# Attention and linear-attention stages of a fused transformer kernel: places of side pieces in two hand-written plans

## The chip, the cores and the metric

One core of a Trainium2 chip runs the whole kernel in one launch. Its engines are TensorE (PE in the profile; PEld is its weight load), the vector engine (DVE), ScalarE (ACT), GpSimd (POOL) and SyncE (SP), which issues most DMA transfers. Each engine works through its own queue in order and waits on semaphores for the others. The metric is the time of one execution on the device in microseconds (us), as the median of the runs shown.

## The reference

The input x is [4, 1024, 128] in float32. It passes six residual blocks, each behind a layer norm:

```
x = x + 0.5 * ffn(layernorm(x), W_r, W_k, W_v, mu_r, mu_k)      # token mix: sigmoid(r) * (relu(k)**2 @ W_v)
x = x + attention(layernorm(x), qkv_w, qkv_b, proj_w, proj_b)   # 16 heads of 8, rotary, softmax over 1024 keys
x = x + 0.5 * ffn(layernorm(x), ...)
x = x + 0.5 * moe(layernorm(x), ...)                            # rms norm, top 2 of 8 experts, hidden 256
x = x + linear_attention(layernorm(x), Wq, bq, Wk, bk, Wv, bv, Wo, bo)
x = x + 0.5 * moe(layernorm(x), ...)

# linear_attention, per head, causal:
q, k = softplus(q), softplus(k)
kv, k1 = cumsum(k[:, :, None] * v[:, None, :]), cumsum(k)
out = (q @ kv) / sum(q * k1)
```

## The kernel before, in words

**Tiles.** The 4096 tokens are 32 tiles of 128. Four tiles make a *group* (512 columns, one PSUM bank), eight a *batch* (one sequence). The stages follow each other: a start (first token mixes, queries of batch 0), attention, the expert loops of the first mixture (r = 0, 1), linear attention, the expert loops of the second (r = 2, 3). x stays in SBUF throughout.

**Attention** (`plan_attention`, line 296) is 256 turns and 2 more to drain. A turn makes scores of four heads by one key tile (TensorE, L979), ScalarE takes the exponential of them in two instructions of 1024 columns (L1257), and the weighted sums of the turn follow two turns later (L994). Scores rotate over six PSUM banks, the weighted sums collect in bank 6, which the vector engine copies out every 16 turns (L1224, "the sums' copy"). What else there is to do is cut into *pieces*, which the planner lays into the turns: queries and keys of the next batch (`norm`, `xt`, `rot`, `split`, `norms`), the bound and the maxima that the exponential needs (`bound`, `max`), values (`val`), division and projection (`div`, `turn`, `proj`, `stats`), the second token mix (`mn`, `mt`, `mk`, `mr`, `mv`, `ms`; `md` and `mx` are its parts on GpSimd and the vector engine), norm factors (`factors`) and the router (`rroot` to `rweight`, then `scat`, the scatters of tokens to expert slots). All products of pieces share one PSUM bank, bank 7, so a product waits until the product before it has been read out.

`turn_of` (line 184) takes the head piece of each of the first two works in the list, and at most one that is a product; a piece ("rest",) fills a turn with nothing. Each engine's queue holds the pieces of a turn in the order of `out`. `attention_queries` (111) puts the i-th `split` of a batch into the turn of another work's product. A split is seven instructions of the vector engine on 128x512 (`dve_attention_side`, line 1067, in batches 1 to 3: square L1096, sums, casts and subtractions L1112, L1113 twice, L1115); they cut the rotated queries or keys into bfloat16 parts. A copy out of the bank of a token mix's transposes is L804 (`mt`). The bound (`attention_maxima`, 141; `dve_bound`, 1167) is a short chain of small vector instructions, then a product (L919), then another.

**Linear attention** (`plan_linear`, 377) is 128 steps and 4 more, 16 to a group of four tiles: a step is one tile by one of four head groups. Scores go to banks 0 to 3 (L1969 and L1965), the mask to lin_scores on the vector engine (L2098), the output to banks 4 and 5 (L1982). All other products take banks 6 and 7 in turn, so each of them waits until the product two before it has been read out. Each step has four lists, issued in this order: *before* (`lnorm`), *state* (`lstate`, the running kv sum, L2045 and L2049 of the vector engine), *out* (one or two pieces of `linear_prepare` and `linear_finish`) and *extra* (the mixture's gathers `gath` and additions `cadd`, `lfac`, router and scatters). `linear_prepare` (159) makes the next group: transposes `lxt` (L597 from `lnorm`'s output), projections `lz` and `lv`, softplus `lexp`, `lln`, sums `lsum`, mask, transposed keys `lkt`. `linear_finish` (174) divides a tile (`ldiv`, L2057 and L2058) and, behind a group's fourth tile, turns it (`lturn`), projects (`lproj`, added to x on GpSimd, L2196) and takes statistics (`lstats`).

`lnorm` normalises the four tiles of a group (`dve_normalise`, L586). `lfac` makes the norm factors of some groups from their statistics (`dve_norm_factors`, L575 to L578, through the Newton steps of `dve_inverse_root`, L561). `route_part` (236) is `rroot` (another inverse root, L1452), `rnorm` (eight tiles scaled, L1463), `rext` (transposes) and `rscore`; `route_slots` (247) is `rtop` (masks of the best two, L1479 to L1488), `rcount` (products L1426 and L1427), `rscan`, `rplace`, `roff`, `rweight`. `spread` (258) lays them out over steps with `ROUTE_TURNS` empty steps behind each kind. From `rplace` on one scatter (L1601, GpSimd) is issued per step.

Of the kernel before, what the change touches and what calls it, by code (L numbers as in the profile page):

```python
# [25 lines left out]
TPB = SEQ // P  # L26
BANK = 512
TPG = BANK // P
# [53 lines left out]
GATHER_STEPS = (9, 4)  # L82
ROUTE_TURNS = {"rroot": 1, "rnorm": 2, "rext": 1, "rtop": 1, "rcount": 1}
PAD = P // HPG
# [56 lines left out]
def attention_maxima(b):  # L141

    yield OTHER, ("rest",)
    yield PRODUCT, ("bound", b)
    yield OTHER, ("rest",)
    yield PRODUCT, ("max", b)
# [27 lines left out]
def linear_finish(u):  # L174
    g, c = divmod(u, TPG)
    yield PRODUCT, ("ldiv", u)
    if c == TPG - 1:
        yield PRODUCT, ("lturn", g)
        yield PRODUCT, ("lproj", g)
        yield OTHER, ("rest",)  # L180
        yield OTHER, ("lstats", g)
# [76 lines left out]
def spread(pieces):  # L258

    out = []  # L260
    for piece in pieces:
        out += [piece] + [None] * ROUTE_TURNS.get(piece[1][0], 0)
    return out
# [32 lines left out]
def plan_attention(k):  # L296
# [11 lines left out]
    for n in range(len(A_STEPS) + A_LAG):  # L308
        out, sums = [], None
        for work in begin.get(n, []):  # L310
            works.insert(len(works) if work[0][1][0] in ("norm", "factors", "mn") else 0, work)
        out = turn_of(works)
        done.update(out)
# [63 lines left out]
def plan_linear(k):  # L377
# [6 lines left out]
    later = {}  # L384
    for at in range(HALF):
        for c in range(TOPK):
            n = GATHER_STEPS[0] * (TOPK * at + c) // GATHER_STEPS[1]
            later.setdefault(n, []).append(("gath", 1, at, c))
        later.setdefault(n + 4, []).append(("cadd", 1, at))
        if at % TPG == TPG - 1:  # L390
            later.setdefault(n + 5, []).append(("cstat", 1, at // TPG))
            if at // TPG % 2:
                later.setdefault(n + 6, []).append(("lfac", 1, at // TPG - 1, 2))
    routes, scatters = [], []
# [10 lines left out]
    for n in range(len(L_STEPS) + L_LAG):  # L405
        before, state, sums = [], None, None
        if n < len(L_STEPS):
# [5 lines left out]
            if not preparing and prepared + 1 < GROUPS and n >= STEPS_PER_GROUP * (prepared - 1) + L_START * HEAD_GROUPS:  # L413
                prepared += 1
                preparing = list(linear_prepare(prepared))
                works.append(preparing)
                before.append(("lnorm", prepared))
            u = g * TPG + c
# [18 lines left out]
        if ("lstats", 1) in out:  # L437
            routes += spread(route_part(2, 0, TPB))
        if ("lstats", HALF_GROUPS - 1) in out:
            routes += [None] * 3 + spread(route_part(2, 1, TPB)) + spread(route_slots(2))  # L440
        if ("lstats", HALF_GROUPS + 1) in out:
            routes += spread(route_part(3, 0, TPB))
        if ("rplace", 2) in extra:
# [2152 lines left out]
```

## Time and profile before

| | |
|---|---|
| runs of the kernel before | 1348.8, 1349.03, 1354.61 us; median 1349.03 |
| the profiled execution's own time | 1345.49 us, with a span of 1343.5 and a granted TensorE clock of 0.899 |
| busy in the span | TensorE 1084.8 us (81%), vector engine 657.9 (49%), ScalarE 807.0 (60%), GpSimd 376.6 (28%) |
| start | 0 to 96.4 us |
| attention | 96.4 to 661.6 us |
| expert loops 0 and 1 | 661.6 to 865.8 us |
| linear attention | 865.8 to 1128.6 us |
| expert loops 2 and 3 | 1128.6 to 1343.5 us |

Times are microseconds unless they are marked ns. A window's row gives a stretch, its length, and the busy time and number of instructions of each engine; PEclk is the TensorE clock that the chip granted in it, as a share of full speed. In a timeline, the bracket behind an instruction is the time that its engine stood idle just before it, and the instruction of another engine that ended the wait. L12 is line 12 of the kernel.

### The profile page before, as it was taken

The page shows a single profiled execution, that of the slowest core. Times are in us where ns is not written, and L with a number is a line of the kernel's source. Part 1 is how long each engine was busy: PE and PEld are TensorE (multiplying, and loading weights), DVE is VectorE, ACT ScalarE, POOL GpSimd, SP SyncE. Part 2 cuts the span into 40 slices and gives each one's busy share as a digit, 9 for nine tenths or more (in the row PEclk, how much of TensorE's full clock was granted, in tenths as well). Part 3 has the DMA queues.
Part 4 walks back from the last instruction along what each step waited for, and adds up shares of the span by engine and source line. Part 5 has one row for each costly group of instructions (what it writes and reads, how often), then busy time and mean ns, then how long its engine had stood idle before and what let it go on. Part 6 is the DMA issues. An engine that isn't in the chain of part 4 may idle for free.

```text
span 1343.5 us, 20969 instructions
## 1 busy us (share of the span) xinstructions
PE 1084.8 (81%) x7616; PEld 504.0 (38%) x7616; DVE 657.9 (49%) x2060; ACT 807.0 (60%) x1164; POOL 376.6 (28%) x376
## 2 busy tenths in 40 slices
PE   3459899899999999999879399787887776898940
PEld 2332222222322321232256256444544344565630
DVE  5752554456355340433165157667666663633522
ACT  4328788688898899989735255644443331464520
POOL 2100111111110102333003643243331263155535
PEclk8679999899999999999999789889888686898975
DMA  4360450432036502100012233100000001143522
GB/s 139 57 96 1 65 90 1 71 57 27 1 56 96 155 1 76 54 15 30 13 40 85 81 87 93 31 17 17 12 14 1 15 33 38 50 118 99 141 66 66
DMA packets 83411, 74.07 MB, mean 55 GB/s; under 512 B 11248, under 2 KB 77680, under 8 KB 82416
## 3 DMA queue, kind: packets, MB, share of 16 engines
q1 hardware_dynamic: 73824, 55.06, 18.8%
q0 software_dynamic: 8192, 16.79, 4.3%
q8 instruction: 66, 1.08, 0.4%
q10 hardware_dynamic: 1296, 0.86, 0.2%
q14 instruction: 33, 0.27, 0.1%
HBM read 39.26 MB, written 33.42 MB: 54 GB/s over the span
## 4 chain that ended last, share of the span: by engine, by line
PE 53%; DVE 20%; ACT 11%; issue 6%; POOL 3%; DMA 2%; another core or an unknown queue 0%; SPq 0%; POOLq 0%; DVEq 0%; ACTq 0%
PE ps L994 11%; PE ps L1666 9%; ACT attn_probs L1257 8%; PE ps L979 6%; PE ps L1692 4%; PE ps L597 3%; PE ps L888 2%; PE ps L1969 2%; POOL moe_back L1611 2%; PE ps L1678 2%; PE ps L1893 1%; DVE lin_scores L2098 1%; PE ps L1656 1%; DVE stats L554 1%; PE ps L1982 1%
## 5 line engine op out<-in xcount | busy, mean ns | idle before, releaser
L1257 ACT ACTIVATE attn_probs<-ps 128x1024 f32<-128x1024 f32 x512 | 485.7, 1075 | 86.0 <-PE ps L979 85.8
L994 PE MATMUL ps<-attn_probs,attn_v 128*18 128x512 f32 x2048 | 273.9, 607 | 5.7 <-DVE room L1224 5.1
L979 PE MATMUL ps<-stack 50*128 50x512 bf16 x1024 | 167.1, 391 | 17.3 <-DMA stack<-row_maxima 11.4
L1601 POOL DMA_INDIRECT slots<-moe_xr,moe_slot x128 | 125.3, 979 | 196.3 <-ACT attn_probs L1257 81.1
L1611 POOL DMA_INDIRECT moe_back<-results,moe_slot x128 | 123.9, 968 | 110.7 <-PE ps L1656 46.8
L1666 PE MATMUL ps<-stack,lin_scores 128*128 x312 | 153.8, 616 | 0.0
L979 PEld LDWEIGHTS ps<-stack 50*128 50x128 bf16 x1024 | 34.1, 94 | 253.6 <-ACT attn_probs L1257 226.3
L1767 ACT ACTIVATE lin_scores<-ps 128x256 f32<-128x256 f32 x156 | 58.6, 382 | 107.0 <-PE ps L1666 101.8
L1740 DVE TENSOR_TENSOR lin_scores<-ps,lin_scores 128x256 f32<-128x256 f32 x156 | 59.0, 418 | 103.5 <-ACT lin_scores L1767 85.2
L1692 PE MATMUL ps<-stack,lin_scores 128*128 x624 | 85.6, 281 | 8.9 <-ACT lin_heads_out L1780 6.8
L1692 PEld LDWEIGHTS ps<-stack,lin_scores 128*128 128x128 f32 x624 | 77.7, 195 | 10.7 <-issue 10.5
L1295 POOL TENSOR_TENSOR room<-room 128x512 f32<-128x512 f32 x16 | 24.5, 1530 | 186.2 <-DVE room L1089 186.2
L1666 PEld LDWEIGHTS ps<-stack,lin_scores 128*128 128x128 f32 x312 | 55.6, 199 | 39.8 <-issue 39.8
L2098 DVE TENSOR_TENSOR lin_scores<-ps,c_causal 128x512 f32<-128x512 f32 x64 | 41.1, 683 | 49.5 <-PE ps L1969 46.8
L1733 DVE TENSOR_SCALAR lin_scores<-ps,c_norm_scale 128x256 f32<-128x256 f32 x80 | 37.8, 473 | 54.1 <-PE ps L1656 48.5
L994 PEld LDWEIGHTS ps<-attn_probs,attn_v 128*18 128x18 f32 x2048 | 34.9, 96 | 75.9 <-issue 46.8
L1089 DVE SCALAR_TENSOR_TENSOR room<-ps,c_attn_b,moe_xr 128x512 f32<-128x512 f32 x32 | 23.9, 748 | 79.9 <-PE ps L888 78.4
L2168 ACT ACTIVATE lin_scores<-ps 128x512 f32<-128x512 f32 x64 | 34.8, 594 | 45.8 <-PE ps L1969 45.5
L1656 PE MATMUL ps<-c_ident,moe_gathered 128*128 128x128 f32 x156 | 33.0, 294 | 30.7 <-DMA moe_gathered<-slots 18.7
L1773 ACT ACTIVATE lin_scores<-ps 128x512 f32<-128x512 f32 x80 | 46.8, 584 | 14.9 <-PE ps L1678 8.4
L1678 PEld LDWEIGHTS ps<-c_ident,lin_scores 128*128 128x128 f32 x312 | 39.0, 143 | 37.5 <-issue 36.3
L888 PE MATMUL ps<-room,c_qk_w 128*128 128x256 f32 x128 | 45.3, 458 | 9.2 <-DVE mix_xt L804 8.8
(237 smaller groups left out, 1567.6 us busy)
## 6 DMA issues: line engine op xcount, KB each, us to landing
stack<-qk_parts SPq DMA_DIRECT2D x48, 256.0 KB, 8.9
moe_gathered<-slots SPq DMA_DIRECT2D x76, 128.0 KB
results<-lin_heads_out SPq DMA_DIRECT2D x76, 128.0 KB
slots<-zeros SPq DMA_DIRECT2D x2, 2496.0 KB, 14.9
qk_parts<-moe_xr SPq DMA_DIRECT2D x32, 128.0 KB, 2.7
qk_parts<-moe_xr SPq DMA_DIRECT2D x16, 192.0 KB, 2.8
stack<-in_expert_w SPq DMA_DIRECT2D x1, 3072.0 KB
x<-in_x SPq DMA_DIRECT2D x8, 256.0 KB, 8.2
```

The source lines that it names most:

```text
L888: instruction = T.matmul(k.ps[:, bank, cols], w[:, 2 * qk + which, :], d.xt[:, half * BANK:(half + 1) * BANK][:, cols], start=True, stop=True)
L979: instruction = T.matmul(k.ps[:, SCORE_BANKS[i % 3][s], :], d.stack[b % 2][rows, 1, pair, kt * P:(kt + 1) * P], d.stack[b % 2][rows, 0, pa ...
L994: instruction = T.matmul(k.ps[32 * j:32 * j + STRIP, PV_BANK, :], d.v[:, b % 2, kt, first:first + STRIP], d.probs[:, n % A_PROBS, j * BANK ...
L1257: A.activation(d.probs[:, n % A_PROBS, 2 * e * BANK:2 * (e + 1) * BANK], k.ps[:, banks[0]:banks[1] + 1, :].rearrange("p a n -> p (a n)"), ...
L1601: G.indirect_dma_start(out=k.dram["slots"][half], out_offset=bass.IndirectOffsetOnAxis(ap=d.slot[:, s, at, c:c + 1], axis=0), in_=d.xr[:, ...
L1611: G.indirect_dma_start(out=k.back[:, at % RING, c, :], out_offset=None, in_=k.dram["results"][half], in_offset=bass.IndirectOffsetOnAxis(a ...
L1666: T.matmul(k.ps[:, bank, :], d.gt[:, u % NB, i, :], w[:, bass.ds(offset[u, i], 2 * HIDDEN)], start=True, stop=True).then_inc(k.full[bank], 1)
L1678: instruction = T.transpose(k.ps[:, bank, at:at + P], d.h[:, u % NB, i, c * P:(c + 1) * P], k.ident[:, :])
L1692: instruction = T.matmul(k.ps[:, bank, i * DIM:(i + 1) * DIM], d.ht[:, u % NB, i, c * P:(c + 1) * P], w[:, 2 * HIDDEN + c * DIM:][:, bass. ...
L1740: V.tensor_tensor(d.h[:, u % NB, i, :], k.ps[:, bank, 0:HIDDEN], d.silu[:, u % NB, i, :], ALU.mult).then_inc(k.free[bank], 1)
L1767: A.activation(d.silu[:, u % NB, i, :], k.ps[:, bank, HIDDEN:2 * HIDDEN], ACT_FN.Silu).then_inc(k.e_silu, 1)
L2098: V.tensor_tensor(d.scores[:, m % NS, :].rearrange("p (j t) -> p j t", j=HPG), k.ps[:, bank, :].rearrange("p (j t) -> p j t", j=HPG), caus ...
```

## The change

In the plan of attention: the pieces of a turn are sorted so that a `split` comes last in it, and `attention_maxima` has a second empty turn ahead of `bound`. In the plan of linear attention: an empty turn ahead of `lturn`; `lnorm` of groups 2 to 7 moves from the step in which its group's preparation begins with `lxt` (12, 30, 46, 62, 78, 94) to the one at which two pieces of the preparation before it are left (10, 27, 43, 59, 75, 91); `lfac` moves from the steps behind the statistics of every second group (two calls of two groups) to steps 30, 58 and 81 (groups 0; 1 and 2; 3); the routers' parts begin `ROUTE_WAIT` = 4 steps behind the statistics they need (before: at once, or 3 steps), with other empty steps between the pieces (`rscore` 0, `rtop` 2, `rext` 1, and none behind `rcount`), and one more ahead of `rtop`. `linear_prepare`, the engines' instructions and all buffers stay as they are. The whole diff:

```diff
--- before.py
+++ after.py
@@ -80,7 +80,8 @@
 L_STEPS = [(g, c, gr) for g in range(GROUPS) for c in range(TPG) for gr in range(HEAD_GROUPS)]
 STEPS_PER_GROUP, L_OUT = TPG * HEAD_GROUPS, (4, 5)
 GATHER_STEPS = (9, 4)
-ROUTE_TURNS = {"rroot": 1, "rnorm": 2, "rext": 1, "rtop": 1, "rcount": 1}
+ROUTE_WAIT, ROUTE_TURNS = 4, {"rroot": 1, "rnorm": 2, "rext": 1, "rscore": 0, "rtop": 2}
+FACTORS_AT = {30: (0, 1), 58: (1, 2), 81: (3, 1)}
 PAD = P // HPG
 
 PRODUCT, SAME_BANK, OTHER = "uses the tensor engine", "goes on with its bank", "uses others only"
@@ -140,6 +141,7 @@
 
 def attention_maxima(b):
 
+    yield OTHER, ("rest",)
     yield OTHER, ("rest",)
     yield PRODUCT, ("bound", b)
     yield OTHER, ("rest",)
@@ -175,6 +177,7 @@
     g, c = divmod(u, TPG)
     yield PRODUCT, ("ldiv", u)
     if c == TPG - 1:
+        yield OTHER, ("rest",)
         yield PRODUCT, ("lturn", g)
         yield PRODUCT, ("lproj", g)
         yield OTHER, ("rest",)
@@ -309,7 +312,7 @@
         out, sums = [], None
         for work in begin.get(n, []):
             works.insert(len(works) if work[0][1][0] in ("norm", "factors", "mn") else 0, work)
-        out = turn_of(works)
+        out = sorted(turn_of(works), key=lambda piece: piece[0] == "split")
         done.update(out)
         b = next_batch
         if b < BATCH and n >= STEPS_PER_BATCH * (b - 1) - BATCH_AHEAD and {("max", b - 1), ("val", b - 1, 1, 1), ("factors", b * TPB, (b + 1) * TPB)} <= done:
@@ -389,8 +392,8 @@
         later.setdefault(n + 4, []).append(("cadd", 1, at))
         if at % TPG == TPG - 1:
             later.setdefault(n + 5, []).append(("cstat", 1, at // TPG))
-            if at // TPG % 2:
-                later.setdefault(n + 6, []).append(("lfac", 1, at // TPG - 1, 2))
+    for n, groups in FACTORS_AT.items():
+        later.setdefault(n, []).append(("lfac", 1) + groups)
     routes, scatters = [], []
     ring = 0
 
@@ -414,7 +417,8 @@
                 prepared += 1
                 preparing = list(linear_prepare(prepared))
                 works.append(preparing)
-                before.append(("lnorm", prepared))
+            elif len(preparing) == 2 and prepared + 1 < GROUPS:
+                before.append(("lnorm", prepared + 1))
             u = g * TPG + c
             u = g * TPG + c
             if gr == HEAD_GROUPS - 1 and (u + 1) % TPB:
@@ -435,11 +439,11 @@
         if routes and (one := routes.pop(0)):
             extra.append(one[1])
         if ("lstats", 1) in out:
-            routes += spread(route_part(2, 0, TPB))
+            routes += [None] * ROUTE_WAIT + spread(route_part(2, 0, TPB))
         if ("lstats", HALF_GROUPS - 1) in out:
-            routes += [None] * 3 + spread(route_part(2, 1, TPB)) + spread(route_slots(2))
+            routes += [None] * ROUTE_WAIT + spread(route_part(2, 1, TPB)) + [None] + spread(route_slots(2))
         if ("lstats", HALF_GROUPS + 1) in out:
-            routes += spread(route_part(3, 0, TPB))
+            routes += [None] * ROUTE_WAIT + spread(route_part(3, 0, TPB))
         if ("rplace", 2) in extra:
             scatters = transfers("scat", 2)
         fill(extra)
```

## Rows read from the trace of the kernel before

**Rows 1.** Windows: a stretch, its length, busy us of PE, PEld, DVE, ACT, POOL, PEclk, DMA.

```profile
96.40:661.60 565.20, 529.75 (x3719) 149.58 (x3715) 239.85 (x699) 492.84 (x530) 95.34 (x84) 0.98 0.24 47
...
865.80:1128.60 262.80, 206.16 (x2124) 118.30 (x2124) 167.98 (x507) 108.05 (x191) 100.34 (x102) 0.83 0.06 18
```

**Rows 2.** Timeline of attention turn 15 to 17: start, us, engine, line, operation, wait before.

```profile
130.13 1.65 POOL L1295 TENSOR_TENSOR room<-room 128x512 f32<-128x512 f32 x1 [7.18 <-DVE room L1089]
...
130.57 1.50 DVE L1112 CAST moe_xr<-room 128x512 bf16<-128x512 f32 x1
...
130.72 0.66 PE L597 MATMUL ps<-c_ident,moe_gathered 128*128 128x128 f32 x4
...
134.36 0.68 DVE L804 COPY mix_xt<-ps 128x512 f32<-128x512 f32 x1
...
138.24 1.02 ACT L1257 ACTIVATE attn_probs<-ps 128x1024 f32<-128x1024 f32 x1 [3.58 <-PE ps L979]
```

**Rows 3.** Timeline of ScalarE, the exponentials behind the splits of turns 22, 59, 65.

```profile
156.41 1.02 ACT L1257 ACTIVATE attn_probs<-ps 128x1024 f32<-128x1024 f32 x1 [2.48 <-PE ps L979]
...
240.46 1.02 ACT L1257 ACTIVATE attn_probs<-ps 128x1024 f32<-128x1024 f32 x1 [3.55 <-PE ps L979]
...
256.37 1.94 ACT L1257 ACTIVATE attn_probs<-ps 128x1024 f32<-128x1024 f32 x2 [3.04 <-PE ps L979]
```

**Rows 4.** Timeline of TensorE, the bound's product in batches 1 and 3.

```profile
188.31 0.41 PE L919 MATMUL ps<-attn_by_head,ones_f 128*128 128x32 f32 x2 [1.73 <-DVE attn_by_head L1183]
...
424.81 0.41 PE L919 MATMUL ps<-attn_by_head,ones_f 128*128 128x32 f32 x2 [2.62 <-DVE attn_by_head L1183]
```

**Rows 5.** Windows of the linear stage, 16 steps each, from step 16 on.

```profile
883.90:913.10 29.20, 24.60 (x284) 13.58 (x276) 20.95 (x58) 14.69 (x26) 13.57 (x14) 0.94 0.08 20
913.10:951.80 38.70, 28.72 (x279) 16.18 (x282) 28.02 (x95) 15.33 (x27) 12.82 (x13) 0.78 0.04 11
951.80:985.50 33.70, 29.68 (x289) 17.28 (x292) 20.75 (x57) 15.22 (x27) 12.32 (x13) 0.85 0.07 17
985.50:1020.90 35.40, 24.59 (x275) 13.82 (x277) 26.57 (x93) 14.74 (x26) 8.87 (x9) 0.89 0.03 6
1020.90:1062.50 41.60, 32.15 (x292) 18.18 (x291) 26.29 (x78) 15.93 (x28) 6.95 (x7) 0.75 0.01 3
1062.50:1094.00 31.50, 23.70 (x273) 13.62 (x276) 22.07 (x65) 14.69 (x27) 19.57 (x20) 0.88 0.09 31
1094.00:1122.50 28.50, 24.06 (x276) 15.05 (x271) 9.70 (x29) 8.19 (x15) 17.94 (x21) 0.86 0.11 36
```

**Rows 6.** Waits of TensorE in the linear stage: waited for, us in total, times, longest.

```profile
PE ps L597 <- DVE room L586: 13.7, 5, 7.3
PE ps L1965 <- DVE lin_scores L2098: 11.6, 8, 4.9
PE ps L597 <- DVE lin_heads_out L2058: 7.5, 8, 3.0
PE ps L1426 <- DVE moe_both L1488: 6.2, 1, 6.2
...
PE ps L597 <- issue: 2.4, 1, 2.4
```

**Rows 7.** Timeline of the vector engine ahead of `lnorm 6`.

```profile
1008.59 0.17 DVE L578 TENSOR_SCALAR ln_var<-moments 128x8 f32<-128x8 f32 x1
...
1015.84 1.11 DVE L586 TENSOR_SCALAR room<-x,moments,ln_rstd 128x128 f32<-128x128 f32 x4
```

**Rows 8.** Windows: steps 20 to 30 of the linear stage, and the five or so behind.

```profile
893.10:910.50 17.40, 14.08 (x162) 8.30 (x162) 16.64 (x47) 8.52 (x15) 8.71 (x9) 0.90 0.06 15
910.50:922.20 11.70, 10.42 (x103) 5.18 (x103) 3.37 (x9) 6.33 (x11) 3.34 (x4) 1.00 0.08 21
```

**Rows 9.** Timeline: the last scatter, and expert loop 2's first product.

```profile
1123.44 0.96 POOL L1601 DMA_INDIRECT slots<-moe_xr,moe_slot  x1 [1.32 <-PE ps L1982]
...
1136.19 0.63 PE L1656 MATMUL ps<-c_ident,moe_gathered 128*128 128x128 f32 x2
```

## The prediction

> **What bounds the kernel now.** The profiled execution spans 1343.5 us and took 1345.49; the runs have a median of 1349.03 (1348.8 to 1354.61). The sum below is made against the profiled execution, which lies 3.5 under the median, and the forecast is the median less the same saving.
>
> I read the busy time by stretch first [rows 1]. The attention stage (565 us) keeps ScalarE busy for 493 with its exponentials: it is the bound there, so a microsecond is saved only where ScalarE stands idle. The linear stage (263 us) has no full engine: TensorE works 206, the vector engine 168, and TensorE's clock is 0.83 of full. Both work through hand-written queues in order, so that stage is bound by waits. Then I read who idles before what.
>
> Attention, turn 15 (the turn of a `split` and the transposes `mt 0`) [rows 2]: TensorE has made the transposes by 131.4, but the vector engine does the split's square, casts and subtractions first (the row of the first cast begins at 130.57), and only at 134.36 copies `mt` out of the one spare PSUM bank. TensorE waits for that bank with `rot`, comes late with the next scores, and ScalarE idles 3.58 us. The same pattern costs 2.48 at turn 22, 3.55 at turn 59 and 3.04 at turn 65 [rows 3]. At turn 81 a wait has another cause: there the copy of the weighted sums stands behind the split, and the product beside it (`mr`) is read by ScalarE. At the bound, TensorE waits 1.73 us (batch 1) and 2.62 us (batch 3) for the short vector chain that makes the bound's operand [rows 4].
>
> Linear stage, by groups of 16 steps [rows 5]: 29.2 us without router work, 38.7, 33.7, 35.4 and 41.6 where chains are laid in, then 31.5 and 28.5. What ends the waits of this stage on TensorE [rows 6]: 13.7 us in five waits for normalised tokens, the longest 7.3 for `lnorm 6`, which is issued in the very step of its transposes `lxt 6`; 11.6 in eight for a score bank that the vector engine frees late, the longest 4.9 in the group from 913.10; 7.5 in eight for the division's output or its bank; 6.2 for `rtop`'s masks, which `rcount` multiplies. The rows of the vector engine show what stood ahead of `lnorm 6` [rows 7]: from 1008.59 the factor chain (2.64 us), then mask, division and root chain (4.6 together), and at 1015.84 `lnorm` itself (1.1). The clock falls with such a wait: the group of the 4.9 has a granted clock of 0.78, that of the 6.2 one of 0.75, the first 0.94 [rows 5].
>
> **The change, part by part.**
>
> *Split last in its turn.* No instruction is added. Turn 15: the copy of `mt` (0.68) ends at 132.1, `rot` no longer waits. The split now runs 132.1 to 135.6 (its seven instructions without the POOL addition of 1.65 us that stretched the first cast to 1.50 [rows 2]); behind it come rotation (about 0.7, as the copy), `mn` (1.1, as `lnorm` in rows 7) and the sums' copy (0.7), which ends near 138.2. TensorE needs it there for its weighted sums of turn 18 and no longer waits: gain 3.7, the idle of 3.58 and a little behind it. Turn 22, without a sums' copy: gain 2.3. Turn 59: gain 3.8, as at turn 15. Turn 65: the sums' copy still stands behind the split, which now begins only after the copy of `mt 3`, so it ends half a microsecond later: loss 0.4; the 3.04 stays. Turns 28 and 78 put the copy of `mk` first, where the next turn is empty on TensorE anyway; the split ends about 2 us later, POOL's square now falls on the cast, and the sums' copies at 33 and 81 come 1 us later: loss 1.0 each.
>
> *Second empty turn.* Its place in the plan decides. For batch 1 it falls beside the division of turn 35: the bound stays at turn 38 directly behind the vector engine's work for `proj`, and its 1.73 stays. For batch 2 `mk 3` fills it, again a copy right ahead of the chain: nothing, at most 0.3 at `max`. All later pieces move by one turn, `mn 4` then stands behind a factor chain and a statistics, and `mt 4` waits 1 us more: loss 1.0. For batch 3 all moves by two to four turns: the bound comes at turn 144 with 2 turns' time for `mn 7` and `mx 6`, and its 2.62 goes. But `split 3 3` now stands at turn 139 behind factors (2.5) and `mn 6` (1.1), and `mt 6`'s copy behind it: TensorE waits 2.5 us at turn 141 and 1.0 at turn 140 instead. Net gain 1.2. The router's chains and scatters move by two turns, where ScalarE does not wait for them: nothing; if that cover were gone, 1 to 2 us.
>
> Sum of attention: 3.7 + 2.3 + 3.8 - 0.4 - 2.0 - 1.0 + 0.3 + 1.2 = 7.9, say 8. Bounds: 12 (the four first waits, 12.6 us, all go) and 3.
>
> One price is open: POOL's subtraction `md` (about 1 us) now starts just as the split's square does. The rows show a cast held 1.50 us beside a POOL addition [rows 2]. The Trainium skill (SBUF — State Buffer, Who interferes with whom) says that an instruction of the vector engine with two SBUF inputs, as the square is, is blocked whole by a GpSimd one that was first; by it turns 15 and 59 would each give about 1 us less and the sum would be 33 instead of 35. The rows agree for the cast; I leave the square free.
>
> *Linear stage.* The empty turn ahead of `lturn` takes away its wait of 0.3 us for the division in seven groups, and puts `proj`'s addition one place back in the vector queue. The first `lsum` comes ahead of it. `lnorm` moves three steps ahead of `lxt`: that wait goes, but `lnorm` (1.03 to 1.1) now stands ahead of the addition that frees the bank for `lkt`, two products later. Two factor chains of two groups become three (1, 2, 1): one chain of 2.64 more. `rroot` and `rnorm` move to steps where the vector queue is short: [rows 8] it is busy 16.64 of 17.4 us in steps 20 to 30 of a group, and 3.37 of 11.7 behind them. `rtop` moves from steps 87 and 89 to 90 and 93, `rcount` from 91 to 96.
>
> I walked each group through both queues in the new order with the durations of the rows; every product waits for the bank of the product two before it. Against [rows 5]:
> - Steps 16 to 31: the vector queue is full from step 20, and the chain of one group at step 30 follows `lxt`. 29.2 becomes 28.2.
> - 32 to 47: `lfac`, `rroot` and `rnorm` are gone from steps 39 to 43. The 4.9, 3.2 for `lnorm 4` (of the 13.7), `rext` (1.0, goes on into the next group) and about 3 of half clock go, 3 us of bank waits return. 38.7 becomes 29.3.
> - 48 to 63: takes in that router work (3 us of TensorE), and at step 58 a factor chain just ahead of `lnorm 5`, so `lkt 4` waits 3.1 for its bank. 33.7 becomes 34.1.
> - 64 to 79: the 7.3, 0.3 and 1 of clock go; behind statistics twice, an add-back and `lnorm` the banks of `lkt` and `lxt` come 2.8 later. 35.4 becomes 29.6.
> - 80 to 95: the 6.2, 1.9 for `lnorm 7` (of the 13.7) and about 3 of half clock go; `lfac` at 81 makes `rext` wait 1.9, and bank waits of 1 return. 41.6 becomes 33.2.
> - 96 to 111: three waits of together 6 behind `rroot` and `rnorm` (the 2.4 that rows 6 put down to issue, and parts of the 11.6 and 7.5) and 2 of half clock go; `rcount` to `rweight` (7 us of vector work) bring 2.7 back. 31.5 becomes 26.2.
> - 112 to 127: half clock at its head goes. 28.5 becomes 25.5.
>
> That is 32.5. A walk does not see every semaphore; I take 27 and keep 33 and 12 as ends. The scatters end 4 steps later: last issue at 1123.44 before, TensorE's first product with their result at 1136.19 [rows 9], 12 us apart; the linear stage's last division, turn and projection cover the delay of some 5 us. If that cover went, 5 us.
>
> Sum: 8 + 27 = 35. Profiled execution 1310.5, median **1314**.
>
> **The rivals.**
>
> *Waits change their place.* In the linear stage the vector engine is full in steps 20 to 30 of each group with or without the change, and what is taken from the head of its queue comes back at `lkt` and `lxt`. For it: 16.64 of 17.4 us [rows 8]. Against it: the 7.3 and 6.2 have whole chains ahead of them that now lie where it is idle 8 of 11.7. Gain then 12 in the linear stage and 5 to 8 in attention: 1331.
>
> *TensorE keeps its clock.* If all groups ran at 0.94 and no bank wait were new, each would come near 28 with its router work: 33 to 35 there and 12 in attention, 1303. For it: in the first group nothing but 4.6 us is idle. Against: `lnorm` stands ahead of the bank's addition. The Trainium skill (TensorE: Matmul & The Clock Gate, HAM oscillation) says that repeated waits bring the engine down to half clock again and again; the clocks of 0.75 and 0.78 in rows 5 agree.
>
> *Slower: the vector queue is the bound of the whole stage.* Then no removed wait counts and what is added does: `lnorm` ahead of the state sum in five groups (5.2), the third chain (2.6), later sums in attention (2.0 + 0.4), the chain ahead of `mt 6` (1), scatters uncovered (5): 16 slower, 1365. It decides once the vector engine is busy in steps 31 to 35 too; it is so for 29% there [rows 8].
>
> *The change does not do what it says* holds in part (the empty turn of batches 1 and 2) and is in the sum; if only the linear half worked, 1322.
>
> **How the numbers follow.** Main case 0.60 (its own range 1305 to 1324), waits change place 0.22, TensorE keeps its clock 0.11, slower 0.03, about no change 0.04. The range reaches from 1301 to 1331: it takes in the main case and most of its neighbours. A measurement of this kernel tells about 0.5% from no change, 6.7 us: faster 0.92, same 0.05, slower 0.03.
>
> **What would show it.** ScalarE's idle of 3.58, 2.48 and 3.55 us gone, that of 3.04 still there or longer; TensorE's wait of 1.73 at the bound of batch 1 still there, a new one of 2 to 3 us at `norms` of batch 3. In the linear stage the 4.9, 7.3 and 6.2 gone, new waits of 1 to 3 us of `lkt` and `lxt` for banks freed by the state sum and division, groups of 26 to 34 us, a granted clock over 0.88. Wrong, if `lkt` waits over 4 us in most groups, if the clock stays at 0.83, or if TensorE waits for the gathered rows at the head of the third expert loop.

## The result and the profile after

The changed kernel takes **1333.61 us** (median of 4 runs, 1330.94 to 1334.21), the kernel before 1349.43 on the same chip. The ratio is 0.9884 with an interval of 0.9862 to 0.9905: faster by 15.8 us, where 35 were forecast; 1333.61 lies 2.6 us above the upper end of the range. The two profiled executions are 1334.21 and 1345.49 us, only 11.3 apart; terms below are read from their traces.

The page of the changed kernel, its head and the costliest group:

```profile
span 1332.3 us, 20939 instructions
...
PE 1076.1 (81%) x7574; PEld 506.0 (38%) x7616; DVE 652.0 (49%) x2073; ACT 806.3 (61%) x1164; POOL 373.7 (28%) x376
...
L1261 ACT ACTIVATE attn_probs<-ps 128x1024 f32<-128x1024 f32 x512 | 485.7, 1074 | 86.0 <-PE ps L983 85.8
```

ScalarE waits 86.0 us ahead of its exponentials, exactly what the page of before shows for that group. So attention has gained nothing as a whole. The windows of its four areas (attention, expert loops 0 and 1, linear stage, expert loops 2 and 3) say where the 11 us are; columns as in rows 1:

```profile
96.50:661.10 564.60, 526.40 (x3701) 148.81 (x3707) 237.24 (x699) 492.71 (x530) 94.83 (x84) 0.98 0.24 48
661.10:868.20 207.10, 163.31 (x838) 107.52 (x840) 104.99 (x367) 94.52 (x219) 71.48 (x74) 0.90 0.24 69
868.20:1117.50 249.30, 200.95 (x2104) 121.66 (x2131) 164.97 (x520) 108.28 (x192) 98.46 (x102) 0.86 0.06 17
1117.50:1332.30 214.80, 144.09 (x745) 97.47 (x745) 83.94 (x256) 80.78 (x195) 92.50 (x97) 0.83 0.31 87
```

With the same edges (first exponential, end of the last one, first output product of the linear stage, and 2.3 to 2.6 us behind the end of its last one) the kernel before has 564.3, 205.1, 265.7 and 212.0. Attention is level, the linear stage gives 16.4, and the expert loops, whose code is the same, take 2.0 and 2.8 back. The 2.8 is no more than two executions of one kernel differ by: the kernel before again (e11) has 215.7 there.

**Attention.** ScalarE's timeline of the changed kernel, behind the splits of turns 15, 22 and 59 (the three that [rows 2, 3] show with 3.58, 2.48 and 3.55 us of idle time), then turns 93 and 99:

```profile
134.53 1.94 ACT L1261 ACTIVATE attn_probs<-ps 128x1024 f32<-128x1024 f32 x2 [0.21 <-PE ps L983]
...
150.42 1.94 ACT L1261 ACTIVATE attn_probs<-ps 128x1024 f32<-128x1024 f32 x2 [0.21 <-PE ps L983]
...
232.15 1.94 ACT L1261 ACTIVATE attn_probs<-ps 128x1024 f32<-128x1024 f32 x2 [0.21 <-PE ps L983]
...
316.77 1.94 ACT L1261 ACTIVATE attn_probs<-ps 128x1024 f32<-128x1024 f32 x2 [4.86 <-PE ps L983]
...
332.57 1.94 ACT L1261 ACTIVATE attn_probs<-ps 128x1024 f32<-128x1024 f32 x2 [3.44 <-PE ps L983]
```

The three waits are gone. By turn 64 the changed kernel is 8.8 us ahead. It loses 4.9 of that at turn 93 and 3.1 at turn 99, where the kernel before did not wait at all. From turn 86 to turn 104 the net loss is 6.6. What stands ahead is seen in the timeline of turns 90 to 93:

```profile
307.44 0.17 DVE L582 TENSOR_SCALAR ln_var<-moments 128x8 f32<-128x8 f32 x1
...
307.64 1.27 DVE L567 TENSOR_SCALAR ln_bits<-ln_var 128x8 int32<-128x8 int32 x1
...
312.10 1.08 DVE L590 TENSOR_SCALAR moe_gathered<-x,moments,ln_rstd 128x128 f32<-128x128 f32 x4
313.10 0.16 DVE L582 TENSOR_SCALAR ln_var<-moments 128x8 f32<-128x8 f32 x1
313.24 1.11 PE L601 MATMUL ps<-c_ident,moe_gathered 128*128 128x128 f32 x4 [3.40 <-DVE moe_gathered L590]
...
315.47 0.69 DVE L808 COPY mix_xt<-ps 128x512 f32<-128x512 f32 x1
...
316.13 1.04 PE L983 MATMUL ps<-stack 50*128 50x512 bf16 x4
```

From 307.44 the vector engine works through `factors 0 8` (begun behind a product, and 3.5 us long), statistics (1.2) and `mn 4` (1.0); TensorE waits 3.40 us for `mn 4` with its transposes `mt 4`. Then the vector engine does `factors 24 32` before it copies `mt 4` out of the spare bank. In the plan before, `mt 4` was issued one turn ahead of `factors 24 32`; the empty turn put both into turn 92, the chain first. Turn 99 is the same kind of thing, in the timeline from 326 on:

```profile
326.49 2.56 DVE L590 TENSOR_SCALAR room<-x,moments,ln_rstd 128x128 f32<-128x128 f32 x4
...
328.98 0.68 DVE L1228 COPY room<-ps 128x512 f32<-128x512 f32 x1
329.11 1.04 PE L601 MATMUL ps<-c_ident,room 128*128 128x128 f32 x4 [1.74 <-DVE room L590]
...
330.80 1.10 DVE L590 TENSOR_SCALAR room<-x,moments,ln_rstd 128x128 f32<-128x128 f32 x4
```

`norm 3 0` is in turn 97 as before, but its transposes `xt 3 0`, which before came at turn 104, now find a free turn at 98, right behind it. They wait for it, and the sums' copy (L1228) stands behind half of it.

Two things make both waits longer than the order alone. GpSimd works beside what stands ahead: the `ln_bits` instruction of `factors 0 8` takes 1.27 us beside an addition of GpSimd from 307.61 to 308.88 (0.17 in e1, where no such addition runs beside it, and 1.26 or 1.27 in e2, e5 and e10), and the first half of `norm 3 0` takes 2.56 beside two instructions of GpSimd, where its second half takes 1.10. This is read from the timelines; no run takes GpSimd's work away there. And behind each wait TensorE's eight products of the weighted sums take 1.91 us instead of 1.05.

**Linear stage**, the windows that answer to [rows 5], groups of 16 steps from step 16 on:

```profile
886.40:913.90 27.50, 22.24 (x276) 13.36 (x275) 21.93 (x70) 14.48 (x26) 13.48 (x14) 1.00 0.08 18
913.90:944.50 30.60, 25.97 (x270) 15.52 (x275) 22.97 (x76) 14.84 (x26) 11.90 (x14) 0.83 0.07 16
944.50:978.50 34.00, 26.90 (x285) 16.26 (x288) 24.28 (x78) 15.92 (x28) 12.85 (x13) 0.94 0.07 17
978.50:1009.40 30.90, 24.70 (x267) 14.24 (x271) 22.04 (x72) 14.72 (x26) 8.50 (x9) 0.89 0.03 8
1009.40:1046.40 37.00, 31.93 (x289) 19.76 (x295) 24.05 (x77) 16.01 (x28) 5.10 (x5) 0.78 0.00 1
1046.40:1072.80 26.40, 22.70 (x266) 13.85 (x271) 22.32 (x67) 13.63 (x25) 12.74 (x13) 0.87 0.06 19
1072.80:1106.40 33.60, 27.27 (x279) 16.86 (x279) 14.59 (x52) 8.69 (x16) 20.10 (x24) 0.85 0.10 35
1106.40:1117.50 11.10, 6.22 (x64) 4.64 (x53) 0.56 (x3) 1.19 (x2) 6.54 (x7) 0.70 0.15 49
```

| steps | before | forecast after | after |
|---|---|---|---|
| 16 to 31 | 29.2 | 28.2 | 27.5 |
| 32 to 47 | 38.7 | 29.3 | 30.6 |
| 48 to 63 | 33.7 | 34.1 | 34.0 |
| 64 to 79 | 35.4 | 29.6 | 30.9 |
| 80 to 95 | 41.6 | 33.2 | 37.0 |
| 96 to 111 | 31.5 | 26.2 | 26.4 |
| 112 to 127 | 28.5 | 25.5 | 33.6 |
| 128 to 131 | 9.0 | (as before) | 11.1 |

Up to step 111 the walk is off by 1.3 us or less in all groups but one, where 3.8 remain. The last group is 8 us too long. The waits of TensorE in the stage answer to [rows 6]:

```profile
PE ps L601 <- DVE lin_total L2053: 7.0, 5, 2.7
PE ps L601 <- DVE lin_heads_out L2062: 5.9, 5, 3.0
PE ps L1969 <- DVE lin_scores L2102: 5.7, 4, 1.9
...
PE ps L1933 <- issue: 4.1, 1, 4.1
PE ps L1933 <- ACT lin_sums L2180: 3.6, 2, 2.9
```

The waits of 4.9, 7.3 and 6.2 us are gone, and new ones of `lkt` and `lxt` for a bank that the state sum frees (7.0 in five) stand in their place, the longest 2.7. Those were in the walk. The 4.1 and 2.9 in the last two rows lie behind step 112 and were not. The kernel before has the like there; these are waits in its steps 112 to 131:

```profile
ACT lin_sums L2176 <- remote: 6.2, 1, 6.2
PE ps L1929 <- issue: 3.6, 1, 3.6
```

"remote" means that nothing of this core that the profile shows ended the wait.

### The profile page after: what moved, and what is told of

It reads as the page before. It is cut to its first block, busy times and chain, and to the rows that moved or that the text cites. A ratio compares the mean times of both kernels' runs of the same rounds, so it can differ in the third digit from the quotient of the medians.

```text
span 1332.3 us, 20939 instructions
## 1 busy us (share of the span) xinstructions
PE 1076.1 (81%) x7574; PEld 506.0 (38%) x7616; DVE 652.0 (49%) x2073; ACT 806.3 (61%) x1164; POOL 373.7 (28%) x376
## 4 chain that ended last, share of the span: by engine, by line
PE 55%; DVE 18%; ACT 10%; issue 6%; POOL 3%; DMA 2%; another core or an unknown queue 2%; SPq 0%; POOLq 0%; DVEq 0%; ACTq 0%
PE ps L998 12%; PE ps L1670 9%; ACT attn_probs L1261 8%; PE ps L983 6%; PE ps L1696 4%; PE ps L601 3%; PE ps L892 2%; PE ps L1682 2%; POOL moe_back L1615 2%; PE ps L1973 2%; DVE lin_scores L2102 2%; PE ps L1986 1%; PE ps L1660 1%; PE ps L1897 1%
## 5 line engine op out<-in xcount | busy, mean ns | idle before, releaser
L998 PE MATMUL ps<-attn_probs,attn_v 128*18 128x512 f32 x2048 | 275.7, 611 | 10.2 <-DVE room L1228 7.3
L1784 ACT ACTIVATE lin_heads_out<-ps 128x256 f32<-128x256 f32 x80 | 30.1, 376 | 39.0 <-PE ps L1696 21.3
```

The source lines that it names most:

```text
L998: instruction = T.matmul(k.ps[32 * j:32 * j + STRIP, PV_BANK, :], d.v[:, b % 2, kt, first:first + STRIP], d.probs[:, n % A_PROBS, j * BANK ...
```

## The experiments

Ratios are to the kernel before, timed on the same chip beside the run. The chips differ: the kernel before took 1329.81 us on the chip of e1 to e4, 1329.38 on that of e5 to e8 and 1348.15 on that of e9 to e12 ("the slow chip" below). So ratios are compared, and stretches of traces.

### e1: split last, alone

```diff
-        out = turn_of(works)
+        out = sorted(turn_of(works), key=lambda piece: piece[0] == "split")
```

> The kernel before with the split sorted to the end of its turn, and nothing else. Theory (sort pays, the extra empty turn loses): ScalarE's waits of 3.6, 2.5 and 3.6 us at turns 17, 24 and 61 fall to 0.2, those of about 1.5 at turns 93 and 0.4 at turn 99 stay as before; the attention stage is 8 us shorter, 1341. Rival (the later vector work of the sorted turns is what makes the new waits of 4.9 and 3.4 us): these two are here, the stage is no shorter at turn 104 than before, 1349.

1317.96 us, ratio **0.9918** (0.9895 to 0.9941). Attention of this kernel, of the kernel before (e11), and of the changed one again (e5), each from its first exponential to its last:

```profile
96.00:650.10 554.10, 522.71 (x3711) 148.52 (x3707) 236.43 (x699) 492.66 (x530) 94.77 (x84) 0.99 0.25 48
```

```profile
95.90:657.30 561.40, 523.36 (x3700) 149.27 (x3707) 239.88 (x699) 492.52 (x530) 95.39 (x84) 0.98 0.24 48
```

```profile
96.40:656.50 560.10, 522.28 (x3701) 148.83 (x3707) 237.38 (x699) 492.63 (x530) 95.05 (x84) 0.98 0.24 48
```

The split alone gains 7.3 us against e11, 10.2 against the first trace of before (564.3) and 10.9 against e3, which has the old plan of attention and ran on the same chip (565.0). Such differences carry 3 to 5 us that have nothing to do with the plan: two traces of one plan can differ by 1.5 us at turn 68 and again at turn 83 (before and e11, the changed kernel and e5, e4 and e1). The waits at turns 17, 24 and 61 are 0.21, turns 93 and 99 have none, as before. The theory holds; the new waits do not come from the sort.

### e2 and e10: the empty turn, alone and for batch 2 only

e2 is the kernel before with one line in `attention_maxima`; e10 has the sorted split, and the line only for batch 2:

```diff
     yield OTHER, ("rest",)
+    yield OTHER, ("rest",)
     yield PRODUCT, ("bound", b)
```

```diff
     yield OTHER, ("rest",)
+    if b == 2:
+        yield OTHER, ("rest",)
     yield PRODUCT, ("bound", b)
```

> The kernel before with the second empty turn ahead of the bound alone. Theory: the pieces of batch 2 and all behind them move by a turn, mt 4 stands behind two factor chains and mn 4 (wait of about 5 us at turn 93), norm 3 0 stands ahead of the sums' copy and xt 3 0 (3.4 us at turn 99); gained are 1.1 at the bound of batch 2 and about 0.5 in batch 3. Net 7 us slower, 1356. Rival (my prediction's step): within 1 us of the kernel before, 1349, with mt 4 only 1 us later.

> The kernel with the split sorted last alone, and the second empty turn only for batch 2. Theory (one turn's shift of mt 4 behind two factor chains and of norm 3 0 ahead of xt 3 0 is the whole loss): waits of 4.9 us at turn 93 and 2 to 3.4 us at turn 99, attention 6 to 8 us longer than with the split alone, ratio 0.997. Rival (the loss adds up from the empty turns of all three batches): under 3 us longer, 0.993.

e2: 1339.93 us, ratio **1.0084** (1.0057 to 1.0110), 10.1 us slower, attention 571.3 us (565.0 in e3 on the same chip):

```profile
95.70:667.00 571.30, 530.97 (x3711) 149.82 (x3707) 240.56 (x699) 492.17 (x530) 95.26 (x84) 0.97 0.24 47
```

It has the wait at turn 93 with 3.32 us, one of 2.1 at turn 99, and one of 6.49 at turn 141: `split 3 3` has come into the turn of `mn 6` and, with nothing sorted, stands ahead of it, so that TensorE waits 5.0 us for `mn 6` at the transposes `mt 6`. e10: 1353.06 us, ratio **1.0027** (1.0005 to 1.0048), against 0.9918 for the split alone. One empty turn in one batch gives all of the gain back. Its two waits, in ScalarE's timeline at turns 93 and 99:

```profile
315.33 1.94 ACT L1259 ACTIVATE attn_probs<-ps 128x1024 f32<-128x1024 f32 x2 [4.86 <-PE ps L981]
331.13 1.94 ACT L1259 ACTIVATE attn_probs<-ps 128x1024 f32<-128x1024 f32 x2 [3.37 <-PE ps L981]
```

They are those of the changed kernel (4.86 and 3.44). The loss between turns 86 and 104 is 6.7 us in e10, 6.6 in the changed kernel's first trace and 6.0 in e5; all kernels with the sorted split and no empty turn lose nothing there. So the rival, that the loss adds up over three batches, falls. e10 ended 0.6% above its expected ratio. Attention was 565.9 us, 11.8 over e1: beside the 6.7 there are 3.2 at turns 67 to 84, of the kind that differs between traces of one plan, and 2.4 behind turn 104. Expert loops 0 and 1, behind it, took 209.7 us against 201.8; e9 and e12, with e1's plan of attention, had 208.2 and 205.4 there on the same chip as e10, so about half or more of that part is no matter of the plan.

### e3: the linear half alone; e4: all but the empty turn; e5: the changed kernel again

e3 is the diff of the change without its two edits of attention; e4 is the changed kernel with this:

```diff
     yield OTHER, ("rest",)
-    yield OTHER, ("rest",)
     yield PRODUCT, ("bound", b)
```

> The whole edit of the linear stage without that of attention. Theory (halves add up): the linear stage is 16 us shorter, its last 20 steps are 5 to 7 us longer than in the kernel before, 1333. Rival (the stalls of the last 20 steps of the changed kernel were chance in one execution): the stage is 23 us shorter, 1326.

> The changed kernel without the second empty turn ahead of the bound. Theory: split last saves 8 and the linear stage 16, nothing is given back at turns 93 and 99: 1325, 8 us under the changed kernel. Rival (the empty turn is neutral and something else costs turns 93 and 99): 1333.

> The changed kernel once more, for its profile beside the others. Theory (sort -10, empty turn +7 to +9, linear half -20, additive): ratio to the kernel before 0.985; its last 20 steps of the linear stage without the long stalls that the first profile shows in them (34 us from step 112 on, not 45). Rival (the stalls belong to the changed plan): 45 us there again, ratio 0.988 or more.

e3: 1309.45 us, ratio **0.9845** (0.9817 to 0.9872). e4: 1302.83, **0.9803** (0.9771 to 0.9835). e5: 1310.73, **0.9864** (0.9829 to 0.9899). Sort, empty turn and linear half multiply to 0.985, the changed kernel has 0.9864 here and had 0.9884 first: the parts add up. e3's and e4's absolute expectations were written for the first chip; their ratios come out at 0.984 and 0.980 instead of 0.988 and 0.982. e3's own trace, on the chip of e1 and e2 (257.1 us in both), has a linear stage of 237.3 us, 19.8 less:

```profile
866.60:1103.90 237.30, 203.24 (x2139) 120.76 (x2136) 165.52 (x522) 108.68 (x192) 95.99 (x100) 0.87 0.06 17
```

Its last 20 steps take 34.2 us at a granted clock of 0.76 in steps 112 to 127, where e1 has 29.0; that is what the theory expected (5 to 7 more), but without the "remote" waits of the first trace. e4's stage, the same step list on the same chip, is 226.3.

The tail of the linear stage in e5, steps 112 to 127 and 128 to 131:

```profile
1066.20:1089.10 22.90, 20.17 (x276) 13.75 (x276) 14.96 (x51) 8.45 (x16) 18.82 (x21) 1.00 0.15 48
1089.10:1094.90 5.80, 4.58 (x69) 3.55 (x62) 1.16 (x5) 1.19 (x2) 4.43 (x6) 1.00 0.15 48
```

28.7 us, where the first trace of the same program has 44.7. On this chip the whole stage is 231.9 us, and 257.1 in e1, which has the old linear plan and ran on another fast chip: 25.2 saved, close to the 27 forecast. Here the gain is taken back elsewhere, at the head of expert loop 2. TensorE's first product there, in e5 and then in e1:

```profile
1104.34 0.69 PE L1660 MATMUL ps<-c_ident,moe_gathered 128*128 128x128 f32 x2 [6.08 <-DMA moe_gathered<-slots]
```

```profile
1112.72 0.44 PE L1656 MATMUL ps<-c_ident,moe_gathered 128*128 128x128 f32 x2 [1.35 <-DMA moe_gathered<-slots]
```

The wait for gathered rows grew from 1.35 to 6.08 us, and loops 2 and 3 from 206.6 to 211.3: the scatters end four steps later in a stage that ends sooner. The other runs on the fast chips agree: 3.7 to 7.1 us of this wait and 209.1 to 211.3 us in the loops with the late scatters (e3, e4, e5, e6, e8), 1.4 and 206.6 to 207.5 with the early ones (e1, e2, e7).

The same step list also does not always take the same time: in e4 it ran in 226.3 us, 5.6 less than in e5. The difference is a clock that fell further in e5 than in e4, in the groups of steps 32 to 47 and 80 to 95. These are the two groups in e4:

```profile
904.60:932.80 28.20, 24.32 (x273) 13.58 (x273) 21.98 (x72) 14.84 (x26) 11.34 (x12) 0.94 0.06 17
...
997.30:1031.30 34.00, 29.56 (x289) 17.61 (x288) 24.28 (x77) 15.92 (x28) 5.10 (x5) 0.87 0.00 1
```

28.2 and 34.0 us at granted clocks of 0.94 and 0.87; e5 has 30.6 and 36.9 at 0.83 and 0.78, the changed kernel's first trace the same as e5, and e3 nearly so. So most of the 3.8 us that were missing in steps 80 to 95 are a fall to the lower of the clock's two levels (1.2 GHz of 2.4), not a wait that the walk had missed. No run tells why e4 was spared it.

The test of the empty turn inside the changed kernel is e4 against e5. They ran on two chips, their intervals touch (0.9835 and 0.9829), and e4's attention took 559.1 us, only 1.0 less than e5's: e4 has the longer waits at turns 39, 68 and 83. Against the changed kernel's first ratio (0.9862 to 0.9905) e4 is apart, and in the turns from 86 to 104 it loses nothing where e5 loses 6.0.

### e6, e7, e8, e12: the parts of the linear edit, each undone in e4

```diff
# e6: lnorm in the step of lxt
+                before.append(("lnorm", prepared))
-            elif len(preparing) == 2 and prepared + 1 < GROUPS:
-                before.append(("lnorm", prepared + 1))
# e7: router as before
-ROUTE_WAIT, ROUTE_TURNS = 4, {"rroot": 1, "rnorm": 2, "rext": 1, "rscore": 0, "rtop": 2}
+ROUTE_TURNS = {"rroot": 1, "rnorm": 2, "rext": 1, "rtop": 1, "rcount": 1}
...
# e8: two chains
-FACTORS_AT = {30: (0, 1), 58: (1, 2), 81: (3, 1)}
+FACTORS_AT = {39: (0, 2), 74: (2, 2)}
# e12: no empty turn ahead of lturn
     if c == TPG - 1:
-        yield OTHER, ("rest",)
         yield PRODUCT, ("lturn", g)
```

> The kernel of the run without the empty turn, with lnorm back in the step of its transposes lxt. Theory (the long wait for lnorm 6 came from the factor and root chains ahead of it, which stay moved): lxt waits 1 to 2 us in five groups, 5 us slower than that run (its ratio was 0.980), 0.984. Rival (the place of lnorm is what removed the 7.3 us wait): a wait of over 4 us at lxt 6 is back and the ratio is 0.990.

> The kernel of the run without the empty turn, with the router's pieces at their old waits and spacings (about four steps sooner). Theory: root chain and eight-tile scaling fall into the full steps of the vector queue, and rcount comes two steps behind the last masks: waits at the score banks of steps 44 to 46 and 76 to 80, and 3 us or more at rcount; 8 us slower than that run, 0.986. Rival (the factor chains' move did it): within 3 us of it, 0.981.

> The kernel of the run without the empty turn, with the factors in two chains (steps 39 and 74, two groups each) in place of three. Theory: group 32 to 47 is 3 us longer, group 64 to 79 2 us longer (a chain straight ahead of lnorm 6), group 48 to 63 3 us and group 80 to 95 1 us shorter: within 2 us, 0.981. Rival (the vector queue's total decides): a chain less makes it 2.6 us faster, 0.978.

> The kernel of the run without the empty turn, without the empty turn ahead of lturn; statistics and router move one step sooner with it. Theory: TensorE waits 0.3 us for the division in seven groups again, the projection's addition stands ahead of the first lsum: 2 us longer in the linear stage, 1 us back from scatters that begin a step sooner: 0.981. Rival (this empty turn is what empties the queue ahead of lkt): 5 us or more longer, 0.985.

| run | median | ratio (interval) | linear stage | loops 2 and 3 |
|---|---|---|---|---|
| e4 | 1302.83 | 0.9803 (0.9771 to 0.9835) | 226.3 | 211.2 |
| e6 | 1305.30 | 0.9826 (0.9789 to 0.9864) | 238.8 | 211.3 |
| e7 | 1298.78 | 0.9766 (0.9732 to 0.9801) | 232.6 | 207.5 |
| e8 | 1299.47 | 0.9764 (0.9729 to 0.9799) | 230.7 | 209.1 |
| e12 | 1318.76 | 0.9783 (0.9760 to 0.9807) | 243.8 (slow chip) | 213.2 |

**e6.** Only the place of `lnorm` differs, and the stage is 7 to 12 us longer than in e5 and e4. `lxt` waits 8.7 us in four groups, in the waits of TensorE in its linear stage:

```profile
PE ps L599 <- DVE room L588: 8.7, 4, 2.9
```

The longest is 2.9 us, not the 7.3 of before: the long one needed the chains ahead of it. The theory has the waits about right (1 to 2 us in five groups expected, 1.65 to 2.94 in four found). By ratio e6 is not told from e4, since their intervals overlap.

**e7** missed its expectation altogether: 0.986 was forecast, 0.977 came. TensorE waits 3.1 us at `rcount` again, though now for a bank that the state sum frees and not for `rtop`'s masks, and the group of steps 32 to 47 takes 33.3 us, so the linear stage is a little longer than in e5. But the scatters start three steps sooner, and loops 2 and 3 take 207.5 us, as with the old plan; its first product there waits 1.43 us for gathered rows:

```profile
1087.41 0.44 PE L1659 MATMUL ps<-c_ident,moe_gathered 128*128 128x128 f32 x2 [1.43 <-DMA moe_gathered<-slots]
```

On the chip as a whole the router's later place earns nothing that these intervals could tell from zero, and may lose. Its group of steps 80 to 95 takes 34.2 us all the same (34.0 in e4, 41.6 before), so most of what the prediction counted there for `rcount` comes without the move. **e8**: two chains or three, no difference that can be told; the order of the groups is as forecast (31.4 for steps 32 to 47, 30.8 for 48 to 63, 32.4 for 64 to 79, 30.8 for 80 to 95). **e12**: no difference that can be told either.

### e9: scatters early

```diff
-            routes += [None] * ROUTE_WAIT + spread(route_part(2, 1, TPB)) + [None] + spread(route_slots(2))
+            routes += [None] * 3 + spread(route_part(2, 1, TPB), SLOT_TURNS) + spread(route_slots(2), SLOT_TURNS)
```

`SLOT_TURNS` has the spacings of before; the rest is e4.

> The kernel of the run without the empty turn, with the second router part and the slots of expert loop 2 (root chain to slot weights) at their old distances, so that the scatters begin three steps sooner; the first part stays four steps later. Theory (the later scatters cost 5 us at the head of expert loop 2): TensorE's wait there for gathered rows falls from 6 to 7 us to 1.4, the last two loops take 207 us and not 211, the linear stage is 227 to 229 us: 5 us faster than the run without the empty turn (0.980) and 2 us faster than the one with the whole router as before (0.977), ratio 0.975. Rival (the router's place in steps 76 to 91 brings back waits of the same size in the linear stage): 0.980.

1317.44 us, ratio **0.9775** (0.9754 to 0.9796), the lowest median on the slow chip and 1.1% under the changed kernel's 0.9884, with intervals that do not touch. But it came to the slow chip, where the wait that it should remove is small anyway (loops 2 and 3 take 213.1 us, 215.7 in e11), so the test of its own point is open: e7 shows that point, not e9. Against e4, e7, e8 and e12 it is not told apart. What beats the changed kernel is what these five share, the missing empty turn in attention.

### e11: the kernel before, again

> The kernel before itself, for its profile beside the others. Theory (the long waits that the first profile has in the last 20 steps of the linear stage belong to that execution or chip and not to the plan): 29 us from step 112 on and not 37.5, linear stage 257 us, last two loops 207, span 1325. Rival (they belong to the plan of before): 37 us there.

1347.23 us, ratio 0.9998 (0.9981 to 1.0015). Its steps 112 to 127 and 128 to 131:

```profile
1091.10:1120.40 29.30, 23.47 (x271) 14.89 (x268) 9.70 (x29) 8.17 (x15) 17.91 (x21) 0.85 0.11 37
1120.40:1128.20 7.80, 7.67 (x61) 5.79 (x61) 1.10 (x4) 1.19 (x2) 0.96 (x1) 0.50 0.28 78
```

37.1 us, as in the first trace of before (37.5); the same linear plan takes 29.0 in e1 and e2, and the changed one 28.7 in e5 against 44.7. All four kernels on the slow chip have a long tail (37.1 to 44.0), and none on the fast ones (28.3 to 34.2, where the longer ones have no such stall but steps at the clock's lower level). My theory said "that execution or chip". The single execution falls, and so does the rival (the plan alone), since the same plan has no such tail on the faster chips. In these traces it goes with the chip, and the plan adds to it: 37.1 to 37.5 with the old plan, 40.2 in e9, 44.0 in e12 and 44.7 in the changed kernel. From step 112 on these plans issue 15, 16, 18 and 19 scatters. Each is a single trace. The timeline of e11 shows such a stall, in which GpSimd goes on and the vector engine does one instruction of 0.20 us:

```profile
1112.83 0.96 POOL L1601 DMA_INDIRECT slots<-moe_xr,moe_slot  x1 [0.31 <-issue]
...
1114.09 0.96 POOL L1601 DMA_INDIRECT slots<-moe_xr,moe_slot  x1 [0.30 <-issue]
...
1116.05 0.60 ACT L2176 ACTIVATE lin_sums<-ps 128x512 f32<-128x512 f32 x1 [6.35 <-remote]
1116.70 1.92 PE L1929 MATMUL ps<-c_head_rows,lin_sums 128*128 128x36 f32 x8 [3.67 <-issue]
```

ScalarE starts a copy 6.35 us after its last work, with nothing of this core named that it waited for, and TensorE's product that reads the copy starts right behind it. The traces of e1 to e8 name no such releaser ("remote") in the linear stage. What it waits for is open; a run on that chip with the scatters taken out of the tail would tell whether they have to do with it, and was not made.

## Why the prediction was wrong

**Split last: right.** The term was 7.4; whole attention stages differ by 7.3 to 10.9 (e1 against e11, before and e3) and by as little as 2.3 (e4 against e11). The turns say it better. Against the first trace of before, the changed kernel gains 8.5 us in turns 16 to 64 and gives 1.4 back by turn 86, for which the forecast had 8.8 and 1.4. Turn 15 went as told: in the changed kernel the split runs from 131.68 to 135.9 (forecast 132.1 to 135.6) and the sums' copy ends at 138.2 (forecast 138.2). The open price came out as taken: the square is 0.68 us long as before, and it is again the first cast that stretches, to 1.25, beside GpSimd's subtraction of 1.41. The Trainium skill (SBUF — State Buffer, Who interferes with whom) says that of an instruction of the vector engine with two SBUF inputs and one of GpSimd that reads SBUF, the one issued first blocks the other whole. The trace agrees: GpSimd's began 0.16 us after the square, and the square kept its 0.68.

**Second empty turn: this step failed.** I wrote "`mt 4` waits 1 us more: loss 1.0" and a net gain of 1.2 for batch 3, +0.5 in all. The traces with it show a loss of 6.0 to 6.7 us between turns 86 and 104 (changed kernel, e5, e10), those without it none. For batch 3, where I had +1.2, the changed kernel loses 1.2 us from turn 112 to 176 in its first trace and gains 0.3 in e5. I had seen that `mn 4` stands behind a chain and missed that `factors 24 32`, with `md 4` before, now shares its turn with `mt 4` and stands between the transposes and their copy out of the bank. And I followed `mt 4` only: `norm 3 0` and `xt 3 0` are pieces of the next batch, which the shift brought from seven turns apart to one. A shift by one turn was priced by its nearest victim; it moves every later meeting of two works.

**Linear stage: the walk was near, the end of the stage was not; this step failed on the chip of the result.** The walk gave 32.5, of which I took 27. On the faster chips it is 19.8 (e3), 25.2 (e5) and 30.8 (e4). On the chip of the result it is 16.4: the last twenty steps, for which the walk had a gain of 3 ("half clock at its head goes"), lost 7.2 (37.5 to 44.7), with stalls that the trace of before shows as well and that the walk left out. That is 10.2 of the 16.1 us that the walk is off. The other 5.8 lie ahead of step 112, 3.8 of them in steps 80 to 95, and these are mostly the clock; the 5.5 that I had taken off the walk cover them.

**Scatters: priced at nothing, with 5 us if the cover went.** It went: 4.7 us on the faster chip (e5 against e1), 2.5 to 4.7 in the five runs with late scatters. I had named it ("if TensorE waits for the gathered rows at the head of the third expert loop"), but the cover had been measured in a stage 25 us longer. On the chip of the result the stalls of the tail left time for the scatters, and the wait is not there.

**The sum.** Against the profiled execution: forecast 8 + 27 + 0 = 35; found 0 + 16.4 - 2.8, less 2.0 in expert loops 0 and 1 and 0.3 elsewhere, = 11.3. By the medians 15.8. The miss is not the slow chip's alone: on e5's chip the same change saves 18.7 us by the medians (1329.38 to 1310.73), with the linear term near its forecast and the empty turn and the scatters against it. The rival *waits change their place* gave 1331, nearest in number; its mechanism did not happen, for steps 32 to 111 gained 22 us. *TensorE keeps its clock* (1303, a ratio of 0.966) came in no run: the lowest ratio is 0.976, and e4's 1302.83 us is near it in number only, on a chip where the kernel before takes 1329.81. *Slower* had the right place in one term, the scatters, and was far off in all.

## What to carry to other kernels

Where a planner deals pieces of several lists into turns, an empty turn is no local edit: print both plans, and for each pair "long vector chain, then a short instruction that frees a bank" compare the distance in turns, for all later works and not just the next. Test such an edit alone; here one line took back what another line had earned, and together they looked like nothing. Compare turn by turn and not stage by stage, since here two traces of one plan differ by up to 5 us in a stage. And when a stage is made shorter, work that was hidden at its end has to be measured against the new length.

## What was not expected of the hardware

- The same program takes 1329 us on some chips and 1348 on others (1.4%). About 8 us of that are in the last 20 steps of the linear stage (29.0 against 37.1), where one scatter per step is issued and ScalarE stands still for up to 6 us with no releaser in the core's own events. Another 5 to 9 are in expert loops 2 and 3 (206.6 and 206.8 us in e1 and e2, 212.0 and 215.7 in the two traces of the kernel before). ScalarE has "remote" waits in the expert loops of all traces from the slower chips (9.6 to 18.7 us at one line) and in none from the faster ones.
- The same attention plan took 554.1 us in five profiles (e1, e6, e7, e9, e12: 553.9 to 554.1) and 559.1 and 559.0 in two (e4, e8), from waits at turns 39, 68 and 83 that differ by 1 to 1.6 us each, with the same instructions ahead of them. The two traces of the kernel before (564.3 and 561.4) and those of the changed kernel (564.6 and 560.1) part at turns 68 and 83 too. No run tells why.
- The linear stage of one plan took 226.3, 231.9 and 237.3 us on fast chips (e4, e5, e3). Between the first two it is the clock in two of its groups; e3 has a clock of 0.76 in steps 112 to 127 besides, where e5 has 1.00.
- A vector instruction on 128x8 int32 took 1.27 us instead of 0.17 beside an addition of GpSimd that had begun 0.03 us before it (at 307.64 in the changed kernel).
